# Two input runs instead of three per stretch, and other waits ahead of the stores that follow them

## What is computed

```
vid = jnp.einsum('bfd,de->bfe', x, W)          # x: 4096 x 32 x 64, W: 64 x 64
idx_i, idx_j = jnp.triu_indices(32, k=1)       # 496 pairs i < j
y = x[:, idx_i, :] * vid[:, idx_j, :]          # 4096 x 496 x 64
```

## Time and profile before

| | |
|---|---|
| time, median of 3 runs | 1284.57 us (1284.52 to 1284.76) |
| the profiled execution: its own time, and its span | 1284.82 us, 1283.2 us |
| VectorE busy | 1086.1 us, 85% of the span, 376 instructions |
| VectorE idle, waiting for stores to land | 125.5 us, 35 times |
| VectorE idle, waiting for TensorE | 30.5 us, 3 times |
| TensorE matmuls busy | 164.1 us, 13%, 256 records |
| DMA | 553.74 MB, mean 432 GB/s |
| mean granted TensorE clock | 0.568 |

### The profile page before, as it was taken

How to read it: one execution, slowest core, us unless ns; L and a number is a source line. 1 busy time by engine, 2 the same in 40 slices (tenths; PEclk the granted TensorE clock), 3 DMA queues, 4 the chain that set the end, 5 groups by cost and what they waited for, 6 DMA issues and landing times.

```text
span 1283.2 us, 1229 instructions
## 1 busy us (share of the span) xinstructions
PE 164.1 (13%) x256; PEld 64.0 (5%) x256; DVE 1086.1 (85%) x376; POOL 0.2 (0%) x4
## 2 busy tenths in 40 slices
PE   2020110203020020030202111003020020302000
PEld 1010000101010010010100000001000000101000
DVE  6898998989889277998899998764899899999960
POOL 0000000000000000000000000000000000000000
PEclk8575665756565555565655656556565565656555
DMA  9999999999999999999999999999999999999999
GB/s 409 443 428 434 438 423 445 431 425 443 439 425 425 425 434 428 442 433 437 425 441 431 437 437 427 429 421 435 437 423 444 433 429 439 435 429 429 441 437 394
DMA packets 10803, 553.74 MB, mean 432 GB/s; under 512 B 1200, under 2 KB 1200, under 8 KB 1584
## 3 DMA queue, kind: packets, MB, share of 16 engines
q1 hardware_dynamic: 9792, 524.29, 94.5%
q10 hardware_dynamic: 1008, 29.43, 5.4%
HBM read 33.62 MB, written 520.09 MB: 432 GB/s over the span
## 4 chain that ended last, share of the span: by engine, by line
DMA 53%; DVE 43%; PE 0%; issue 0%; SPq 0%; DVEq 0%
DMA out_dram<-mem 46%; DVE mem L197 43%; DMA mem<-in_r_x_dram 6%; PE vid L257 0%; SPq L222 0%; DVEq L195 0%
## 5 line engine op out<-in xcount | busy, mean ns | idle before, releaser
L197 DVE TENSOR_TENSOR mem<-mem,vid 128x1024 f32<-128x1024 f32 (+13 forms) x376 | 1086.1, 2962 | 156.4 <-DMA out_dram<-mem 125.5
L257 PE MATMUL vid<-mem 128*128 (+1 forms) x256 | 164.1, 803 | 1011.7 <-PEq L256 1011.7
L257 PEld LDWEIGHTS vid<-mem 128*128 128x128 f32 x256 | 64.0, 262 | 1110.9 <-issue 1110.9
L364 POOL MEMSET const-bfloat16-1.0<- 128x1 bf16 x1 | 0.1, 103 | 0.0
L364 POOL MEMSET const-uint8-127<- 128x1 uint8 x1 | 0.1, 103 | 0.0
L364 POOL MEMSET const-float32-1.0<- 128x1 f32 x1 | 0.1, 100 | 0.0
L364 POOL MEMSET const-float32-0.0<- 128x1 f32 x1 | 0.1, 99 | 0.2 <-issue 0.2
## 6 DMA issues: line engine op xcount, KB each, us to landing
out_dram<-mem SPq DMA_DIRECT2D x12, 7680.0 KB, 24.6
out_dram<-mem SPq DMA_DIRECT2D x7, 7168.0 KB, 20.8
out_dram<-mem SPq DMA_DIRECT2D x2, 6656.0 KB, 27.3
mem<-in_r_x_dram SPq DMA_DIRECT2D x2, 1408.0 KB, 43.5
mem<-in_r_x_dram ACTq DMA_DIRECT2D x1, 1408.0 KB, 30.1
mem<-in_r_x_dram SPq DMA_DIRECT2D x2, 640.0 KB, 41.5
mem<-in_L_rec_W_x_dram ACTq DMA_DIRECT2D x1, 1088.0 KB, 5.6
mem<-in_r_x_dram ACTq DMA_DIRECT2D x1, 1024.0 KB, 7.7
```

The costliest lines, as they stand in the source:

```text
L197: self.engine.tensor_tensor(*operands, MULT).then_inc(self.dve, 1)
L257: nc.tensor.matmul(vid[:, b * BANK : b * BANK + BANK, :], lhsT=w, rhs=mem[:, bass.ds(k * step + (first + b * BANK), BANK), :], start=True, ...
L364: nc = _bacc.Bacc("TRN2", target_bir_lowering=False, num_devices=1, dynamic_dma_scratch_size=256)
```

## The change

In each of the three stretches the runs of 128, 10 and 22 fields become two runs, of 124 and 36 fields (the head keeps its run of 16 ahead of them). The bytes, their order within a stretch and their places in memory stay; four fields and the run of 10 join the last run.

The hold ahead of slot 0's store goes; that store waits for one more product of VectorE instead (product 7 rather than 6). The hold ahead of slot 22's and slot 42's store is now always the count of TensorE's banks: the first bank of the stretch's first tile, number 49 for tile 6 and number 89 for tile 11.

```diff
-HEAD = range(6), [(16, 16), (286, 128), (414, 10), (424, 22)]
+HEAD = range(6), [(16, 16), (286, 124), (410, 36)]
 STRETCHES = [
-    (range(6, 11), [(32, 128), (22, 10), (0, 22)]),
-    (range(11, 16), [(286, 128), (414, 10), (424, 22)]),
+    (range(6, 11), [(36, 124), (0, 36)]),
+    (range(11, 16), [(286, 124), (410, 36)]),
 ]
...
-    held = stretch(act, *HEAD, "h")[-2], 16
+    stretch(act, *HEAD, "h")
+    held = None
...
                 q = sp if slot < SP_SLOTS else act
-                q.after_products(done)
+                q.after_products(done + (slot == 0))
...
                     sp.after(stored[-2])
-                    landed = stretch(sp, tiles, runs, f"g{slot}_")[-2]
-                    held = (landed, 16) if len(runs) > 2 else (pe, tiles[0] * (F // BANK) + 1)
+                    stretch(sp, tiles, runs, f"g{slot}_")
+                    held = pe, tiles[0] * (F // BANK) + 1
```

## The result

The changed kernel takes 1293.63 us (median of 6 runs, 1293.17 to 1294.07), beside 1284.72 us of the kernel before in the same comparison. The ratio is 1.0068, with a 95% interval of 1.0058 to 1.0079: 8.9 us slower. The profiled execution took 1294.03 us, with a span of 1292.6 us, 9.4 us longer than before. VectorE works as long as before (1086.0 us), and the bytes are the same.

A forecast was written before the change was run, and what follows sets the result against it. The prediction took the DMA engines, 99.9% held, as the bound. Terms +8.2 (slot 22), 0 (slot 42), 0 (slot 0) and -0.1 (fewer DMAs) gave +8.1 on 1284.57: 1292.7 us, 8-in-10 range 1290.3 to 1295.0.

The forecast's parts named there:

- What bounds the kernel: Whole span: the two queues hold the 16 DMA engines 99.9% at 432 GB/s; VectorE's 85% is not the bound.
- Slot 22's hold: Near 468 us: store issued at 474.6 instead of 465.07, queue empty meanwhile, landing 8.2 us later (7.2 to 9.2).
- a delay that is smaller at the end: Sign of being wrong: a delay at 490 us that is smaller at the kernel's end.
- The 388 GB/s: Kernel before, 468.10 to 475.70 us: the rate moved there, taken as what falls out when the queue is empty.
- The clock's term: Around bank 49: TensorE at 2.4 instead of 1.2 GHz would save 1.0 us; taken as 0, -1.0 kept for the range.
- Slot 42's hold: Near 875 us: store moves to 874.2, still covered by the run of 36 until about 876; cost 0 (to 0.3).
- Slot 0's hold: In the head: store issued at 28.70, not 29.75, finding the engines busy; cost 0, both ends within 0.1 us.
- Three DMAs less: All three stretches: a DMA in a full queue costs some 0.05 us beyond its bytes; -0.1 us (-0.3 to 0).
- The rival of fewer DMAs: Each dropped DMA gives back at most 3.0 us and no queue runs empty: 1275.6 us; chance 0.03.
- The fit of about 2.0 us: Skill's DMA time: about 2.0 us plus bytes at 436 GB/s; would give back 6 us, forecast 1286.8.
- The cover of 36 fields: Rival: at the holds the run of 36 moves as long as the store waits; 1284.5 us, no change; chance 0.07.

The follow-up runs named there:

- VectorE early: The changed kernel with product 146 cut from 80 fields to 16; 1285.11 us beside 1284.76 us of the kernel before.
- bank 49 alone: The kernel before with one edit: slot 22's store waits for TensorE's bank 49, not the run of 10's landing; 1293.61 us beside 1284.78.

## Why the prediction was right, step by step

*What bounds the kernel* held: the DMA engines are full everywhere but in one slice, and the time lost is the time that they were empty. 99.9% was the right place to start from, since it says that no such time is made good later.

*Slot 22's hold* held, with its mechanism: VectorE's product 148 sets bank 49, the bank sets the store. The issue was forecast for 474.6 and came at 474.65 with this hold alone. Cutting product 146 shows that VectorE's lateness is the cause and not the wait on TensorE. The size, +8.2 by landing, came out well partly by luck, since two errors met. A store in an empty queue needs 19.55 us instead of the forecast 20.2, that is 1.35 us beyond its bytes and not 2.0; this made the landing 7.6 us late. But the landing was the wrong measure: the time moved by 8.8, about as much as the queue was behind in bytes. The landing follows the slowest of the 16 engines, and the empty time counts on all of them: the average engine ended the store 8.5 us later. The prediction named a delay that is smaller at the end as a sign of being wrong; it was larger. The 388 GB/s that the prediction took for what falls out was blurred by the edges of its stretch, since 0.4 us further on the same trace has 459. The clock's term stayed 0: bank 49 took 2.07 us at 0.50 again.

*Slot 42's hold* at 0 held, alone and in the changed kernel. *Slot 0's hold* at 0 held for the time, but not in its detail. The store was issued at 28.90, near the forecast 28.7, but I had said that its landing stays within 0.1 and that all rows up to 465 us stay within 0.2. VectorE's product that waits for that landing started 1.2 us later in the changed kernel (51.23 against 50.04 us), and product 143 0.8 us later (443.67 against 442.85). Of the four executions with this head, three had the first of these products 0.6 to 1.2 us later than before; the fourth, with VectorE early, had them at 49.89 and 442.94. The head alone cost no time that can be told.

*Three DMAs less* at -0.1 can't be told from 0. The rival of fewer DMAs, with up to 9 us of gain, is refuted: the runs alone, which drop two of the three DMAs, gain nothing. The fit of about 2.0 us that the prediction cites beside it (the Trainium skill, DMA: Bandwidth & Descriptors, Anatomy of one DMA) is headed there as that of DMAs issued by GpSimd, while SP and ScalarE issue these. What I had missed is that runs and hold belong together. The landing of the run of 10 was a mark in time, 3.3 us ahead of the last landing; without that run the next earlier landing comes too early, at a cost of about 1 us that can hardly be told, and the count that replaced it comes too late in the first stretch.

*The cover of 36 fields* as a rival fell in the first stretch and holds in the second, as its condition said: with product 148's end at 463.7 instead of 472.1, ahead of the 464.6 that it asked for, it holds in the first stretch too.

## What to carry to other kernels

Where the DMA engines are the bound, ask of every wait ahead of a store what is still in the queue when it ends; the cost here was the time that the queue was empty, about one for one, and it was not made good. A count of an engine is as good a hold as a landing only where that engine is early, so look at the same wait in each place where it stands: here it cost nothing that can be told at 875 us and 8.8 us at 468. Before a small transfer is merged into a larger one, ask who uses its landing as a mark.

## What the runs showed of the hardware

A store issued behind queued loads slowed the last of these loads. With slot 22's store issued about 17, 6 and 3.3 us ahead of the last load's landing (at 453.7 without a hold, at 463.2 held by the first run, at 465.07 before), the run of 22 took 4.8, 4.1 and 3.3 us from the landing ahead of it, and its packets held the 16 engines for 4.29, 3.95 and 3.38 us. All three holds together are worth 1.65 us of time (0.3 to 2.7 by the interval). The slowing is not the same each time: a run of 36 with the store 5.7 us ahead took 5.7 us, and 6.4 with it 6.4 us ahead, where the changed kernel needed 44.1 + 0.4 - 39.0 = 5.5. Why a queued store does this, and from which distance on, the runs leave open.

A store that found the queue empty needed 19.55 us from issue to landing in three kernels, 1.35 us more than its 7.86 MB need at 432 GB/s. With bank 49 alone it was issued at 474.65, and the first packet on each engine started 0.8 to 1.0 us later.
